# Two layers of cross attention: the second layer's queries as three fp32r products, with the low part made on GpSimd

## The reference

```python
# layer 0, 16 heads of 16
h = concatenate([ctx, x], axis=1)
q = x @ q_w + q_b;  k, v = split(h @ kv_w + kv_b)
attn = softmax(where(mask, q @ k.T / 16, -inf)) @ v
a = attn @ out_w + out_b + x
o = a * rsqrt(mean(a**2) + 1e-6) * postnorm_w
X1 = gelu(o @ mlp_w1 + mlp_b1) @ mlp_w2 + mlp_b2 + x
# layer 1, 8 heads of 64; X1 is read as [channel 64, position 256]
xn = (X1 - mean) * rsqrt(var + 1e-5) * gamma + beta      # over channels and positions
q = Wq @ xn + bq;  k, v = split(Wkv @ ctx + bkv)
att = softmax((q * c**-.25) @ (k * c**-.25))             # 256 x 256 for each head
out = X1 + Wo @ (att @ v) + bo
```

## Time and profile before

| | us |
|---|---|
| median of 3 runs | 602.5 (601.56, 602.5, 603.3) |
| profiled execution | 603.94 |
| its span, first to last instruction | 602.0 |
| TensorE busy | 570.4 (95%) |
| VectorE busy | 547.9 (91%) |
| ScalarE busy | 504.4 (84%) |
| GpSimd busy | 420.8 (70%) |

### The profile page before, as it was taken

How to read it: one execution, slowest core, us unless ns; L and a number is a source line. 1 busy time by engine, 2 the same in 40 slices (tenths; PEclk the granted TensorE clock), 3 DMA queues, 4 the chain that set the end, 5 groups by cost and what they waited for, 6 DMA issues and landing times.

```text
span 602.0 us, 21122 instructions
## 1 busy us (share of the span) xinstructions
PE 570.4 (95%) x8564; PEld 463.7 (77%) x8564; DVE 547.9 (91%) x1053; ACT 504.4 (84%) x1904; POOL 420.8 (70%) x419
## 2 busy tenths in 40 slices
PE   4799999999999999999999999999999999998976
PEld 4689877777888787887888777887877777876755
DVE  5977889999999999999899989998999999999996
ACT  2848779988899987998899888998989897968873
POOL 2643468777588767796777865886676985787764
PEclk9779999999999999999999999999999999999989
DMA  8213001011102111111111111011111111110110
GB/s 285 76 38 103 22 19 55 20 37 30 35 29 57 43 38 28 38 56 32 33 46 55 38 38 27 31 35 29 37 29 38 32 38 40 37 29 20 40 24 23
DMA packets 50080, 26.45 MB, mean 44 GB/s; under 512 B 38048, under 2 KB 48320, under 8 KB 49984
## 3 DMA queue, kind: packets, MB, share of 16 engines
q1 hardware_dynamic: 49984, 25.11, 15.3%
HBM read 22.99 MB, written 2.10 MB: 42 GB/s over the span
## 4 chain that ended last, share of the span: by engine, by line
PE 64%; DVE 23%; ACT 6%; POOL 4%; DMA 2%; issue 1%; SPq 0%
PE bank L671 60%; DVE E1b L1179 6%; DVE nm L1162 5%; PE bank L792 4%; POOL E1b L1445 3%; ACT E1b L1362 3%; DVE nm L1017 2%; DVE E L1027 2%; DMA mski<-in_msk 1%; DVE QS L1155 1%; ACT E L1259 1%; DVE PT L1035 1%; DVE hm L1099 1%; ACT hm L1333 1%; DVE mrow L989 1%; PE bank L822 1%
## 5 line engine op out<-in xcount | busy, mean ns | idle before, releaser
L1445 POOL TENSOR_TENSOR E1b<-E1b,rs 128x512 f32<-128x512 f32 x255 | 264.0, 1060 | 85.4 <-DVE rs L1168 80.4
L1362 ACT ACTIVATE E1b<-bank,nm 128x256 f32<-128x256 f32 x512 | 237.0, 495 | 28.6 <-DVE nm L1162 28.4
L1162 DVE TENSOR_REDUCE nm<-bank 128x2 f32<-128x512 f32 x256 | 164.2, 674 | 9.4 <-PE bank L671 9.0
L1179 DVE STREAM_TRANSPOSE E1b<-E1b 128x1024 f32<-128x1024 f32 x128 | 155.9, 1227 | 5.7 <-POOL E1b L1445 4.8
L671 PE MATMUL bank<-ctx,QS 64*128 64x256 f32 x1024 | 134.5, 394 | 1.7 <-DVE PT L1035 1.0
L671 PE MATMUL bank<-E1b,CT 32*64 32x256 f32 (+1 forms) x4224 | 120.9, 375 | 10.2 <-ACT E1b L1362 3.6
L671 PEld LDWEIGHTS bank<-E1b,CT 32*64 32x64 f32 x4224 | 95.4, 132 | 30.4 <-ACT E1b L1362 5.1
L1362 ACT ACTIVATION_READ_ACCUMULATOR E1b<-bank,nm 128x1 f32 x512 | 116.7, 228 | 0.0
L671 PEld LDWEIGHTS bank<-ctx,QS 64*128 64x128 f32 x1024 | 91.6, 186 | 25.5 <-issue 6.8
L1259 ACT ACTIVATE E<-bank,nm 128x128 f32<-128x128 f32 x256 | 90.7, 409 | 9.6 <-DVE nm L1017 9.6
L1259 ACT ACTIVATION_READ_ACCUMULATOR E<-bank,nm 128x1 f32 x256 | 63.8, 249 | 0.0
(11 more groups left out here) (119 smaller groups left out, 823.1 us busy)
## 6 DMA issues: line engine op xcount, KB each, us to landing
CT<-in_hT SPq DMA_DIRECT2D x256, 32.0 KB, 1.9
hraw<-in_hT SPq DMA_DIRECT2D x8, 512.0 KB, 3.4
ctx<-in_ctx SPq DMA_DIRECT2D x32, 128.0 KB, 2.7
xnat<-in_xn SPq DMA_DIRECT2D x8, 256.0 KB, 2.8
E1b<-in_w SPq DMA_DIRECT2D x2, 1024.0 KB, 8.8
out<-y SPq DMA_DIRECT2D x16, 128.0 KB, 1.7
E1b<-in_kvw SPq DMA_DIRECT2D x2, 256.0 KB, 4.6
mski<-in_msk SPq DMA_DIRECT2D x32, 1.0 KB
```

Source lines behind the costliest of these rows:

```text
L1162: e.tensor_reduce(nm1[:, u % 16, :], bank[place["S", u]][:, :].rearrange("p (i t) -> p i t", i=2), AX.X, ALU.max, negate=True).then_inc(dv ...
L1179: e.transpose(E1b[:, k:k + 2, :, :], E1b[:, k:k + 2, :, :]).then_inc(dve_steps, 1)
L1362: t = e.activation(E1b[:, r, i, :], bank[bk][:, i * 256:(i + 1) * 256], ACT.Exp, bias=nm1[:, r, i:i + 1], scale=1.0, accum_out=sum1[:, r, ...
L1445: e.tensor_tensor(E1b[:, u % 16, :, :], E1b[:, u % 16, :, :], rs1[:, u % 16, :].unsqueeze(2).to_broadcast([128, 2, 256]), ALU.mult).then_i ...
```

## The change

The normed tokens are written as an fp32r high part `xh` (two buffers). A new step xl on GpSimd computes them once more in f32 into `xt` and subtracts the high part, which gives the low part `xl` (one buffer). MM is split once, in Mg, into `MH[0]` and `MH[1]`. The query step waits for xl and issues three fp32r products in place of each f32 product. The planner gets xl with its cost, and a new cost for q.

The final sum of a pair is written over X1 instead of into y1, so that the DMA of the output reads X1, with four semaphores, and step X1 waits for the output of two groups before. The step o0 writes its half straight into AO (tmpo is gone) and o1 adds to it there. The bias row obt is kept in place of `sm("ob")`. MM lies in slot 3 of E1b and the staged output weights in QS[2]. `WIN`, `HEADAT`, `PREP`, `LATE`, `STAY`, `PREFER` and every entry of `SHIFT` have new values; Yh, Zh, zh, qs and xl have entries for the first time.

```diff
-WIN = (-48.4, 20.6)
-HEADAT = -484
-PREP = 16
-LATE = (-2, -12.75, 11, -4.25, 0.25, -1.75, 5.5, 8.75)
-STAY = dict(full=0, rows=0.6, grid=2, cols=1.5, rows32=1.5, cols32=0)
-PREFER = (0, 2)
+WIN = (-48.9, 19.5)
+HEADAT = -607
+PREP = 19
+LATE = (-3, -1.75, 16, 15.25, 6.5, 2.25, 10.25, 3.25)
+STAY = dict(full=0.3, rows=1.5, grid=2, cols=1.5, rows32=0.6, cols32=0)
+PREFER = (0, -0.5)
...
-    "var": (130, 300), "q": (853, 1100), "S": (860, 1050), "Z": (3700, 3900), "Y": (1715, 1950),
+    "var": (130, 300), "q": (690, 940), "S": (860, 1050), "Z": (3700, 3900), "Y": (1715, 1950),
...
-            [("fin", 2 * (g - 2) + i) for i in range(2)] if g >= 2 else []), empties=(("W2", g, 0), "other"))
+            [("out", 2 * (g - 2) + i) for i in range(2)] if g >= 2 else []), empties=(("W2", g, 0), "other"))
...
-            [("q", p - 2, c) for c in range(2)] if p >= 2 else [("obtd",), ("wlo", 3)]))
+            [("q", p - 2, c) for c in range(2)] if p >= 2 else []))
+        add("xl", p, on=G, at=at, after=[("xn", p)] + ([("q", p - 1, c) for c in range(2)] if p else []))
         for c in range(2):
-            add("q", p, c, on=V, at=at + 0.5 + c, after=[("xn", p), ("Mg",)],
+            add("q", p, c, on=V, at=at + 0.5 + c, after=[("xl", p), ("Mg",)],
...
-                    w.wait_ge(*last([("xn", p), ("Mg",)]))
+                    w.wait_ge(*done("xl", p))
+                    w.wait_ge(*done("Mg"))
                     for i in range(2):
                         pr = 2 * c + i
-                        for a, bk in ((0, pa), (64, pb)):
-                            t = mm(bk[:, i * 256:(i + 1) * 256], MM[a:a + 64, pr * 128:(pr + 1) * 128],
-                                   xnrm[p % 2][a:a + 64, :], i == 0, i == 1)
+                        for k, (x, y) in enumerate(((0, 0), (0, 1), (1, 0))):
+                            for a, bk in ((0, pa), (64, pb)):
+                                t = mm(bk[:, i * 256:(i + 1) * 256], MH[x][a:a + 64, pr * 128:(pr + 1) * 128],
+                                       (xl if y else xh[p % 2])[a:a + 64, :], i == 0 and k == 0, i == 1 and k == 2)
...
-                    e.tensor_scalar(MM[:, :], MM[:, :], sm("gamma"), None, ALU.mult).then_inc(dve_steps, 1)
+                    t = own(e.tensor_scalar(MH[0][:, :], MM[:, :], sm("gamma"), None, ALU.mult))
+                    w.wait_ge(dve_own, t)
+                    e.scalar_tensor_tensor(MH[1][:, :], MM[:, :], sm("gamma"), f(MH[0][:, :]), ALU.mult,
+                                           ALU.subtract).then_inc(dve_steps, 1)
...
+                    if g >= 2:
+                        for u in range(2):
+                            w.wait_ge(d_out[(2 * g + u) % 4], 16 * ((2 * g + u) // 4))
...
-                    if p and runs["xn", p - 1] == "ACT":
-                        w.wait_ge(*done("xn", p - 1))
+                    if p:
+                        w.wait_ge(*done("xl", p - 1))
...
-                    if p >= 2:
-                        w.wait_ge(d_out[p % 2], 16 * (p // 2))
-                    e.scalar_tensor_tensor(y1[p % 2][:, :], bank[place["Y", p]][:, 0:256], cbias[:, 0:1],
+                    e.scalar_tensor_tensor(X1[p % 4][:, :], bank[place["Y", p]][:, 0:256], cbias[:, 0:1],
                                            X1[p % 4][:, :], ALU.add, ALU.add).then_inc(dve_steps, 1)
...
-                    if back(g, c, 1):
-                        w.wait_ge(*done("o1", *back(g, c, 1)))
-                    e.activation(tmpo[:, :, :, :], o[:, :, :, 0, :], ACT.Copy, bias=0.0,
+                    if g:
+                        w.wait_ge(*done("sq", g - 1))
+                    e.activation(AO[:, :, 2 * c:2 * c + 2, :], o[:, :, :, 0, :], ACT.Copy, bias=0.0,
...
+                elif name == "xl":
+                    p, = key
+                    w.wait_ge(*done("xn", p))
+                    e.tensor_scalar(xt[:, :], X1[p % 4][:, :], mu[:, 0:1], rstd[:, 0:1], ALU.add, ALU.mult).then_inc(pool_own, 1)
+                    own[0] += 1
+                    w.wait_ge(pool_own, own[0])
+                    if p:
+                        w.wait_ge(*last([("q", p - 1, 0), ("q", p - 1, 1)]))
+                    e.tensor_tensor(xl[:, :], xt[:, :], f(xh[p % 2][:, :]), ALU.subtract).then_inc(pool_steps, 1)
```

More of the change, by code:

```diff
@@ L261, in slot @@
         return [("Z", u // 8 - 2)]
-    return ([("wlo", x) for x in range(3)], [("M",), ("WS",), ("uu",)], [("w2l", k) for k in range(4)], [("w1l", k) for k in range(4)])[u // 4]
+    return ([("wlo", x) for x in range(3)] + [("Mg",)], [("M",), ("WS",), ("uu",)], [("w2l", k) for k in range(4)], [("w1l", k) for k in range(4)])[u // 4]
 def plan():
@@ L389, in plan @@
                 add("qe", n, c, on=P + A, at=at + 0.5 + c + 4 * (n % 2), after=[("q", p, c), ("uue",)] + (
-                    [("S", 8 * (n - 3) + 4 * c + 2 * i) for i in range(2)] if n >= 3 else []),
+                    [("S", 8 * (n - 3) + 4 * c + 2 * i) for i in range(2)] if n >= 3 else [("obtd",), ("wlo", 3)] if n == 2 else []),
                     empties=(("q", n, c), "other"))
@@ L434, in plan @@
                         banks=[] if j else [("Y", p)], kind="other")
-            add("fin", p, on=A, at=at, after=[("Y", p) if n < NB - 1 else ("Yh", p, 1), ("out", p - 2) if p >= 2 else None, ("uue",)],
+            add("fin", p, on=A, at=at, after=[("Y", p) if n < NB - 1 else ("Yh", p, 1), ("uue",)],
                 empties=(("Y", p), "other"))
@@ L478, in build @@
         w2 = [sb(f"w2{i}", [128, 8, 256], F32R) for i in range(2)]
-        MM = sb("MM", [128, 512])
+        MH = [sb(f"MH{i}", [128, 512], F32R) for i in range(2)]
         WS = sb("WS", [128, 256])
@@ L520, in build @@
         rstd = sb("rstd", [128, 1])
-        xnb = sb("xnb", [128, 2, 256])
-        xnrm = [xnb[:, i] for i in range(2)]
+        xh = [sb(f"xh{i}", [128, 256], F32R) for i in range(2)]
+        xl = sb("xl", [128, 256], F32R)
+        xt = sb("xt", [128, 256])
         QS = [sb(f"QS{i}", [128, 4, 256]) for i in range(3)]
@@ L529, in build @@
         rs1 = sb("rs1", [128, 16, 2])
-        sto = xnb[:, :, :]
+        sto = QS[2][:, 0:2, :]
+        MM = E1b[:, 3].rearrange("p m k -> p (m k)")
         stk, stq = E1b[:, 0:2], E1b[:, 2]
@@ L534, in build @@
         l1w = E1b[0:64, 4:8, :, :].rearrange("p w a n -> p w (a n)")
-        y1 = [sb(f"y1{i}", [128, 256]) for i in range(2)]
         def f(ap):
@@ L1047, in _ @@
                     w.wait_ge(*done("obt"))
-                    e.tensor_tensor(obt[:, :], bank[place["obt",]][:, 0:256], sm("ob"), ALU.add).then_inc(dve_steps, 1)
+                    e.tensor_tensor(sm("ob"), bank[place["obt",]][:, 0:256], sm("ob"), ALU.add).then_inc(dve_steps, 1)
                 elif name == "Me":
@@ L1144, in _ @@
                         w.wait_ge(*last([("q", p - 2, 0), ("q", p - 2, 1)]))
[L1145 to L1147 removed]
+                    e.tensor_scalar(xh[p % 2][:, :], X1[p % 4][:, :], mu[:, 0:1], rstd[:, 0:1], ALU.add,
                                     ALU.mult).then_inc(dve_steps, 1)
@@ L1154, in _ @@
                         w.wait_ge(*last([("S", 8 * (n - 3) + 4 * c + 2 * i) for i in range(2)]))
+                    if n == 2:
+                        w.wait_ge(*done("obtd"))
+                        w.wait_ge(*done("wlo", 3))
                     e.tensor_tensor(QS[n % 3][:, 2 * c:2 * c + 2, :],
```

33 lines of the change are left out of this document (12 added, 21 removed), and 142 rows, old and new, of tables (COST, SHIFT).

## The result

| | kernel before | changed kernel |
|---|---|---|
| median | 602.75 us, 4 runs | 611.08 us, 4 runs |
| lowest to highest | 601.56 to 603.3 | 607.52 to 613.18 |
| profiled execution's span | 602.0 | 605.6 |

The ratio is 1.0135, 95% interval [1.0077, 1.0193]. The change costs some 8 us; 598.1 was predicted. The same changed kernel measured again with the experiments, as after_again, gave 1.0128 [1.0101, 1.0155]. The profiled execution took 607.52 us, the shortest of its four: with 0.983 it had a higher granted clock than the two long ones (612.83 us at 0.972, 613.18 at 0.975). The profiled execution before (603.94 us) was longer than its median, so the two profiles are 3.6 us apart where the medians are 8.3 apart. What follows from one trace is therefore checked against others of the same order.

The account below looks back on a forecast made before the run. TensorE was taken to bound the long middle, VectorE next. Products -5.0, edges +1.6, engine sharing +0.4 and new order -1.4 summed to -4.4 us, giving 598.1 us; range 591.5 to 603.5, leaving out a tenth on each side.

Parts of the forecast that it names:

- Pace of the products: Queries on TensorE: 24 fp32r products take 1.42 us a pair instead of 1.73, saving 0.31 us a pair.
- loads in series: TensorE's query weight loads run one after another: 2.6 us a pair, +13 us, 615.5; chance 0.03 (loads or products).
- Low part in the middle, buffers: GpSimd's low part, 1.42 us a pair, hidden in the middle; in-place sum and moved buffers also cost nothing.
- A microsecond taken from TensorE should come off the end: Middle, 82 to 548 us: TensorE is busy 458.25 of 466 us, so its savings should shorten the run.
- The -5.0 us of the sum: Query blocks on TensorE: 0.31 us saved in each of 16 pairs, at best 6.9 us in all.
- the second rival: Middle: VectorE's in-order queue, 94% busy, passes on half of TensorE's gain, giving 600.3 us; chance 0.15.
- The new order ... -1.4 us, with 3 us either way: New due times of all steps: gain of an eighth of TensorE's 11 us idle in the last stretch.
- I therefore cost the middle at nothing: Middle pairs: xl's delay to the queries is covered by the lead; without cover up to 2.5 us a pair.
- the longer lead: Planner's preparation of pairs: PREP 19 instead of 16 heads, 3 heads being 6 us, to cover xl's delay.
- the rival's +8 for half of the pairs: Low part late behind GpSimd's normalizations: half of 16 pairs wait 1.0 us, +3 net, 605.5 us; chance 0.11.
- Edges +1.6 us: First and last query blocks, without cover: xl's delay less the faster block, 1.1 us each, first half covered; 0 to 2.5.

Follow-up runs that it names:

- c6: Changed code in the exact order of the kernel before, without xl, one f32 product of the high parts; buffer edits kept: 603.22 us, ratio 1.0005.
- a2: Changed kernel in its own order, three fp32r products, xl cut to one 128x1 operation, second product rereading the high part: 611.36 us, ratio 1.0132.
- c5: Changed code in the exact order of the kernel before, without xl, three fp32r products, the second rereading the high part: 602.03 us, ratio 0.9981.
- c7: Order of the kernel before, no xl, a single fp32r product per block instead of three: 603.59 us, ratio 1.0016.
- a3: Changed kernel in its own order, one f32 product per block of the high parts, xl cut to one 128x1 operation: 611.63 us, ratio 1.0144.
- e2: Kernel before, with the 1 MB load of w1 issued ahead of the tokens and mask of group 1: 605.26 us, ratio 1.0044.
- d1: Changed kernel, with VectorE taking the mask of group 1 behind group 0's first row maxima: 608.25 us, ratio 1.0092.
- e1: Changed kernel, with the 1 MB load of w1 issued behind the tokens and mask of group 1: 609.38 us, ratio 1.0108.
- e4: Changed kernel with both head edits, w1 behind the mask's load and VectorE taking the mask behind the row maxima: 608.42 us, ratio 1.0095.
- c1: Whole change in the order of the kernel before, xl inserted on GpSimd where the old plan ends xn: 617.86 us, ratio 1.0253.

## Why the prediction was wrong

- **Pace of the products: right.** 1.42 us a pair predicted in place of 1.73, 1.59 against 1.92 measured from start to the next product. With 64x128 loads between them the products keep a full-height product's pace in both halves. The Trainium skill (TensorE: Matmul & The Clock Gate, section LDWEIGHTS (loading the stationary operand)), read as loads in series, would have given an estimated 2.6 us; the block of 1.59 us above decides for the row against that reading.
- **Low part in the middle, buffers: right.** The durations came within a tenth, but for the first pair's, no X1 waits for an output; c6 puts the buffers at nothing; a2 against the changed kernel puts the low part in its own order at nothing.
- **"A microsecond taken from TensorE should come off the end": wrong.** The -5.0 us of the sum were work, and their value was -1.2 (c5 against c6, and no more than 3), and 0 for 14 us in c7, where the clock took part of it back. It was read from the earlier trace rows, a busy share of 98% and a chain share of 64%. Both describe which engine is full, not which is waited for once the order is fixed; the second rival ("VectorE takes over", half of the gain passed on) came nearest, and even it was on the generous side.
- **"The new order ... -1.4 us, with 3 us either way": wrong, and the largest error.** It is +9 us (a2 against c5, a3 against c6), half to three quarters of it at the edges: some 2 from one 1 MB load issued ahead of the tokens and the mask of group 1 (2.5 in e2; d1, e1 and e4 with 1.5 either way), 2 to 4 in the tail, the rest in the middle, where no single place was found. Every load has a new due time too; the prediction priced the order by the tail's idle time alone and looked at no queue of the head. The earlier trace rows showed only that the first 82 us have gaps; the row that would have warned, mrow's wait of 1.33 us for its mask, was in the trace and not read.
- **"I therefore cost the middle at nothing": right as a number, wrong as a cost.** The lateness of xl was rightly bounded (up to 2.5 us a pair with the cover gone; 16.4 us in 11 waits in c1, the longest 3.3), and the longer lead does hide it. But the cover was an order, and the order that gave xl its room lost time elsewhere. The low part costs 15.8 us without the new order and 9 through it. Had the two been priced as one, with the rival's +8 for half of the pairs as the middle, the forecast would have been on the slower side.
- **Edges +1.6 us: too small.** The last low part is done 3.5 us after the kernel before began these queries, where 1.1 were counted: the high part is 1.1 us later, and GpSimd takes 2.5 us from there, with a multiply ahead of the two operations that the edge's term left out. The first queries start at 84.98 us, against 81.71. The new wait of a pair's statistics for xl stood in the diff (`done("xl", p - 1)`) and had no term; it costs 6.1 us of VectorE's time in c1 and is not seen as a wait in the changed kernel.

Summed again with what was measured: products -1.2, order with the low part in it +9, buffers +0.5, together +8.3, as in the medians, since the parts were taken from them.

## What to carry to other kernels

When every engine's order is fixed, measure the exchange rate before promising a gain: leave the work out and see what comes off the end; here 14 us of the busiest engine were worth nothing. Look at the granted clock too, since an engine with less to do can have the lower one. A step added to a full queue costs its place even when it is tiny (4.5 of 15.8 us here), and it can close a chain (xl between one pair's statistics and the next). A newly computed order is a change by itself: run the new code in the old order and the old work in the new order, and look at the first 20 us of DMA issues, where one reordered load cost 2.5 us.

## What the runs showed of the hardware that was not expected

- Transfers of 1 KB issued behind large ones came late. With the mask of group 1 issued at 8.9 us, behind 2 MB of weights and the tokens, VectorE got it at 17.95 us; issued at 7.49, behind 1 MB and the tokens, at 15.61. With two loads ahead, e2 gave 19.93.
- The same wait does not always cost the same clock. In six profiles of the new order TensorE waits 2.13 or 2.14 us ahead of the late Z; the products behind it then took 3.71 us at full clock in the changed kernel, after_again and d1, but 5.40 us in a2, e1 and e4, at a granted clock of 0.83 for 555 to 565 us in e1. Here is the row of e1:

```profile
556.12 5.40 PE L691 MATMUL bank<-E1b,CT 32*64 32x256 f32 x128 [2.14 <-ACT E1b L1387]
```

These 1.7 us may be part of why executions of the changed kernel lie between 607.5 and 613.2 us; that was not shown.
- A delay in the first 20 us need not arrive in full. e2's first maxima are done 4.3 us later than in the kernel before (22.86 against 18.54), but its granted clock is 0.80 from 20 to 45 us, against 0.66, and its first Z starts only 1.2 us later.
